# Half of a bf16 normalisation is moved from VectorE to GpSimd in an attention and expert kernel

## The chip, the cores and the metric

The kernel runs on all 8 cores of one Trainium2 chip. Each core takes one of the 8 batch entries (2048 tokens by 1024 features) with its own copy of the weights, and the cores exchange nothing. The metric is the device time in microseconds of the slowest core. The version before takes 1118.87 us (median of 3 runs, 1118.42 to 1119.35).

A core has TensorE (matmuls, PE in the profile), VectorE (DVE), ScalarE (ACT), GpSimd (POOL) and SyncE (SP, here only a DMA queue). They run their own instruction lists and meet at semaphores.

## What is computed

`x` is normalised over its features, and the result `xn` feeds two branches whose outputs are added to `x`:

```python
xn = layernorm(x)                                  # per token, over 1024 features
# branch 1: linear attention
q, k, v = split(xn @ w_qkv.T + b_qkv)              # 16 heads of 64
q = silu(q);  k = softmax(k, over tokens)
out = q @ (k.T @ v)                                # per head
out = layernorm(out) * sigmoid(gate(xn))
out = out @ w_out.T + b_out
# branch 2: 8 experts, top 2 by router logits xn @ Wr.T, capacity 769 tokens for each expert
y = x + out + sum over the chosen experts e of  w_e * (xn @ We[e])
```

## The kernel before

One function, `program(me, eng)`, is run once for each engine. It walks through the whole kernel in one order and emits only what belongs to the engine `me`, so the order of each engine's instructions is the order of the source. Helpers `mm` (TensorE, line 167), `dve` (VectorE, 177), `act` (ScalarE, 184), `gps` (GpSimd, 191) and `dma` (198) count the instructions, each of which raises its engine's semaphore when done; the parameter `inc` makes no difference in `dve`, `act` and `gps`. Each `dve`, `act` or `gps` instruction also waits until the one before it on its own engine has completed, and each `dma` until the one before it on its own queue has landed. `w(owner, ctr, val)` makes the engine `owner` wait for the counter `ctr`: "dv" is VectorE's, "gp" GpSimd's, "pe" TensorE's, "ac" ScalarE's, "d1" to "d3" the DMA queues.

The feature-major copy of `x` (8 chunks of 128 features by 2048 tokens) lies in `ar3` as bf16 (`xhi`). The stages, in order:

1. Load `x` and sum `x` and its square over the features by matmuls with a column of ones; router logits from `xhi` and a remainder `xlo3`.
2. Mean and 1/deviation of each token, as rows of 2048 numbers on one partition (`srow`, `qrow`, `crow`, `drow`). Then `reps[:, 0, :]` (scale) and `reps[:, 1, :]` (shift) are those rows spread to 128 partitions.
3. **The normalisation** (lines 342 to 352): for each of 4 blocks `tb` of 512 tokens and each of 8 chunks `h`, two VectorE instructions on 128x512 bf16: `tmpb = xhi * scale`, then `xn = tmpb + shift`. 64 instructions. `tmpb` and `tmpb2` are the two halves of the small tile `scr_b` (128x1024); `xn` lies in `ar1`, `xhi` in `ar3`.
4. **The routing chain**. TensorE transposes the logits into bank 4 and sums the router weights into bank 6. VectorE copies the two out (`lraw`, `wrsum`), and these copies stand behind the normalisation in VectorE's list. TensorE then waits for both copies, makes one small matmul (`wrsum` spread over partitions) and goes on to K.
5. **K projection**: 16 token tiles `tc` of 128 tokens, each as 2 banks of 9 matmuls (8 with `xn` as the stationary operand, one for the bias). A tile waits for its token block of `xn` by `t_xn_tb[tc // 4]`. ScalarE takes the exponential out of PSUM.
6. V projection, K^T V, Q projection, gate hidden layer, attention output, second layernorm, gate, output projection; then 8 experts of 256 matmuls each.
7. GpSimd adds `x` to each finished token tile (128x1024, f32), and ScalarE's queue writes it to `y`.

On GpSimd's queue the last four DMAs ahead of stage 3's end are `wk_t`, `wv_t`, `wg1_t` and `wg2_t`. Behind them stands a clearing of `scr_b` that waits for the whole normalisation, then a small memset, and then nothing until the load of `wq_t`, which waits for the end of K.

Of the kernel before, what the change touches and what calls it, by code (L numbers as in the profile page):

```python
# [9 lines left out]
ALU = mybir.AluOpType  # L10
# [4 lines left out]
HC = 8  # L15
# [7 lines left out]
def build_nc():  # L23
# [24 lines left out]
    with contextlib.ExitStack() as ctx:  # L48
# [31 lines left out]
        reps = sb("reps", [128, 2, 2048], BF16)  # L80
        scr_b = sb("scr_b", [128, 1024], BF16)
        tmpb = scr_b[:, 0:512]
        tmpb2 = scr_b[:, 512:1024]
# [40 lines left out]
        with nc.psum_tensor("PS", [128, 4096], F32) as PS:  # L124
# [8 lines left out]
            def bank(b, lo=0, hi=512):  # L133
                return PS[:, 512 * b + lo: 512 * b + hi]

            xn = ar1[:].rearrange("p (c t) -> p c t", c=HC)
            xhi = ar3[:].rearrange("p (c t) -> p c t", c=HC)
# [17 lines left out]
            def program(me, eng):  # L155
                c = {"pe": 0, "dv": 0, "ac": 0, "gp": 0, "d1": 0, "d2": 0, "d3": 0}
# [4 lines left out]
                def w(owner, ctr, val=None):  # L161
                    if me == owner:
                        eng.wait_ge(S[ctr], c[ctr] if val is None else val)

                def mm(out, l, r, start, stop, inc=False):
                    if me == "tensor":
                        i = eng.matmul(out, l, r, start=start, stop=stop)  # L167
                        if inc:
                            i.then_inc(S["pe"], 1)
                    if inc:  # L170
                        c["pe"] += 1
                    return c["pe"]

                def dve(name, *a, inc=True, **k):
                    if me == "vector":
                        eng.wait_ge(S["dv"], c["dv"])  # L176
                        getattr(eng, name)(*a, **k).then_inc(S["dv"], 1)  # L177
                    c["dv"] += 1
                    return c["dv"]

                def act(name, *a, inc=True, **k):
                    if me == "scalar":
                        eng.wait_ge(S["ac"], c["ac"])
                        getattr(eng, name)(*a, **k).then_inc(S["ac"], 1)  # L184
                    c["ac"] += 1
                    return c["ac"]

                def gps(name, *a, inc=True, **k):
                    if me == "gpsimd":
                        eng.wait_ge(S["gp"], c["gp"])  # L190
                        getattr(eng, name)(*a, **k).then_inc(S["gp"], 1)  # L191
                    c["gp"] += 1
                    return c["gp"]
# [84 lines left out]
                for h in range(HC):  # L278
                    for tb in range(TB):
                        sl = slice(512 * tb, 512 * (tb + 1))  # L280
# [35 lines left out]
                for which, rowsrc in ((0, drow), (1, crow)):  # L316
                    for tb in range(TB):
                        if which == 1 and tb == 0:
                            w("tensor", "dv", t_rows)
                        if t_reps_toks:  # L320
# [3 lines left out]
                           inc=True)  # L324
# [5 lines left out]
                t_reps = c["dv"]  # L330
# [10 lines left out]
                               ALU.subtract)  # L341
                t_xn_tb = []
                w("vector", "dv", t_reps)
                for tb in range(TB):
                    sl = slice(512 * tb, 512 * (tb + 1))
                    for h in range(HC):
                        dve("tensor_tensor", tmpb[:, :], xhi[:, h, sl],
                            reps[:, 0, sl], ALU.mult, inc=False)
                        dve("tensor_tensor", xn[:, h, sl], tmpb[:, :],
                            reps[:, 1, sl], ALU.add, inc=(h == HC - 1))  # L350
                    t_xn_tb.append(c["dv"])
                t_xn = c["dv"]
                w("gpsimd", "dv", t_xn)
                t_kvz = gps("memset", scr_b[:, :], 0.0)

# [54 lines left out]
                for tc in range(NT):  # L410
                    for ob in range(2):
                        idx = tc * 2 + ob
                        bnk = idx % 4
                        if idx == 0:
                            w("tensor", "dv", t_lgt_ev)
                            w("tensor", "d2", t_wk)
                        w("tensor", "dv", t_xn_tb[tc // 4])
                        if idx >= 4:
                            w("tensor", "ac", tok_k[idx - 4])
                        for h in range(HC):  # L420
                            mm(bank(bnk), xn[:, h, 128 * tc:128 * (tc + 1)],
                               wkv[:, 0, h, 512 * ob:512 * (ob + 1)],
                               start=(h == 0), stop=False)
                        mm(bank(bnk), ones_b[0:1, 0:128],
                           bk_sb[:, 512 * ob:512 * (ob + 1)], start=False,
                           stop=True, inc=True)
                        tk = c["pe"]
                        w("scalar", "pe", tk)
                        tok_k[idx] = act("activation",
                                         expK[:, tc, 512 * ob:512 * (ob + 1)],  # L430
                                         bank(bnk), AF.Exp)
# [11 lines left out]
                   inc=True)  # L443
# [12 lines left out]
                for tc in range(NT):  # L456
# [30 lines left out]
                    inc=False)  # L487
# [17 lines left out]
                for ch in range(HC):  # L505
# [12 lines left out]
                    for tc in range(NT):  # L518
                        mm(bank(b2, 0, 1), expK[:, tc, 128 * ch:128 * (ch + 1)],
                           ones_c_b[:, 0:1], start=(tc == 0), stop=(tc == NT - 1),  # L520
                           inc=(tc == NT - 1))
# [134 lines left out]
                for which, rowsrc in ((0, drow), (1, crow)):  # L656
                    for tb in range(TB):
                        if t_reps2_toks:
# [3 lines left out]
                           inc=True)  # L662
# [10 lines left out]
                for oc in range(HC):  # L673
                    for tb in range(TB):
# [16 lines left out]
                        sl = slice(512 * tb, 512 * (tb + 1))  # L691
# [17 lines left out]
                for tc in range(NT):  # L709
                    for ob in range(2):  # L710
# [8 lines left out]
                        for h in range(HC):  # L719
# [5 lines left out]
                           inc=True)  # L725
# [21 lines left out]
                for e_i in range(E):  # L747
                    src = accA if e_i % 2 == 0 else accB
                    dstv = accB if e_i % 2 == 0 else accA
                    for tc in range(NT):  # L750
                        for ob in range(2):
# [7 lines left out]
                            for h in range(HC):  # L759
# [3 lines left out]
                                   inc=(h == HC - 1))  # L763
# [31 lines left out]
            with nc.Block() as block:  # L795
                @block.tensor
                def _(eng):
                    program("tensor", eng)

                @block.vector  # L800
                def _(eng):
                    program("vector", eng)

                @block.scalar
                def _(eng):
                    program("scalar", eng)

                @block.sync
                def _(eng):
                    program("sync", eng)  # L810

                @block.gpsimd
                def _(eng):
                    program("gpsimd", eng)
# [44 lines left out]
```

## Time and profile before

| | |
|---|---|
| time, median of 3 | 1118.87 us |
| the profiled execution's own time | 1118.52 us |
| its span on the slowest core (core 2) | 1116.6 us |
| TensorE matmul busy | 874.3 us (78%) |
| VectorE busy | 453.2 us (41%) |
| ScalarE busy | 103.6 us (9%) |
| GpSimd busy | 58.0 us (5%) |
| spans of the eight cores | 1111.9 to 1116.6 us |
| mean granted TensorE clock, die 0 and die 1 | 0.864 and 0.866 |

The span runs from the first to the last instruction of the core; 1.9 us of the profiled execution's time lie outside it. A share of busy time is a mean over stages with different limits, so the rows further below are read stage by stage. GpSimd's durations are rough.

### The profile page before, as it was taken

Reading aid. Unit: us, or ns where it says so; the run is one execution under the profiler, and the core shown is the slowest. Engines: PE = TensorE matmul, PEld = TensorE weight load, DVE = VectorE, ACT = ScalarE, POOL = GpSimd, SP = SyncE. Lnnn points to the kernel's source line nnn. Section 1 sums busy time; section 2 is a strip of 40 time slices with the busy share of each in tenths; the row PEclk is TensorE's granted clock in tenths of the full one; section 3 lists DMA queues with packets and bytes.
Section 4 is the critical chain, followed back from the end, with each engine's and each line's share of the span. In section 5 each row is a group of like instructions: output and inputs, shape, how many; then the busy total and the mean of one; then the engine's idle time right before and its main releaser. Section 6 shows DMA issues by size and latency. Waiting matters only on the chain.

```text
span 1116.6 us, 11121 instructions; the slowest of 8 cores (1111.9 to 1116.6 us)
## 1 busy us (share of the span) xinstructions
PE 874.3 (78%) x3848; PEld 358.6 (32%) x3914; DVE 453.2 (41%) x692; ACT 103.6 (9%) x123; POOL 58.0 (5%) x58
## 2 busy tenths in 40 slices
PE   2338109999959995605549999999999999999992
PEld 0003003333353331101003334444444444444441
DVE  1248672023320007276763334444444444444441
ACT  1221002220002210512220000000000000000000
POOL 1011000000000000000000000000000000000244
PEclk8669559999958995855559999999999999999996
DMA  6844600030040022000000040404040404040376
GB/s 133 217 104 76 123 0 1 1 60 16 1 77 1 1 36 40 0 0 1 0 0 1 1 75 1 75 2 76 1 76 1 76 1 76 1 76 1 95 236 235
DMA packets 23300, 55.59 MB, mean 50 GB/s; under 512 B 4752, under 2 KB 4752, under 8 KB 22224
## 3 DMA queue, kind: packets, MB, share of 16 engines
q0 software_dynamic: 16160, 29.68, 16.5%
q1 hardware_dynamic: 4208, 12.63, 3.8%
q10 hardware_dynamic: 2880, 12.58, 3.0%
q8 instruction: 33, 0.54, 0.2%
q14 instruction: 19, 0.16, 0.0%
HBM read 76.18 MB, written 8.39 MB: 76 GB/s over the span
## 4 chain that ended last, share of the span: by engine, by line
PE 64%; DVE 17%; DMA 11%; issue 4%; ACT 2%; DVEq 1%; POOL 0%; POOLq 0%; ACTq 0%
PE PS L167 64%; DMA ar<-x_fm 6%; DMA y<-fpool 5%; DVE scr_b L177 5%; DVE ar L177 5%; DVE srow L177 3%; DVE reps L177 1%; ACT bpool L184 1%; DVE qrow L177 1%; ACT qrow L184 1%; DVEq L176 1%; DVE drow L177 0%; DVE crow L177 0%; DVE bpool L177 0%; DVE fpool L177 0%
## 5 line engine op out<-in xcount | busy, mean ns | idle before, releaser
L167 PE MATMUL PS<-ar 128*128 128x512 bf16 (+1 forms) x3135 | 700.0, 378 | 25.9 <-DVE ar L177 9.2
L167 PEld LDWEIGHTS PS<-ar 128*128 128x128 bf16 x3200 | 304.0, 100 | 386.3 <-issue 56.1
L177 DVE SCALAR_TENSOR_TENSOR ar<-PS,lc,ar 128x512 bf16<-128x512 f32 x256 | 192.2, 751 | 251.0 <-PE PS L167 251.0
L177 DVE CAST ar<-PS 128x512 bf16<-128x512 f32 x96 | 66.4, 692 | 94.2 <-PE PS L167 90.2
L167 PE MATMUL PS<-ar,ones_c_b 128*1 128x512 bf16 x64 | 23.2, 500 | 57.5 <-ACT bpool L184 57.2
L184 ACT ACTIVATE ar<-PS 128x512 bf16<-128x512 f32 x64 | 38.2, 597 | 93.7 <-PE PS L167 93.7
L198 POOL DMA_DIRECT2D ar<-we x8 | 7.0, 876 | 672.4 <-PE PS L167 672.4
L177 DVE TENSOR_TENSOR ar<-fpool,ar 128x2048 bf16<-128x2048 f32 x8 | 18.3, 2292 | 56.5 <-DMA ar<-x_fm 28.3
L167 PE MATMUL PS<-bpool,wg_sb 64*128 64x512 bf16 x32 | 18.7, 584 | 28.4 <-DVE ar L177 28.4
L167 PE MATMUL PS<-drow,ones_b 1*128 1x512 bf16 x8 | 4.4, 554 | 44.1 <-DVE crow L177 35.2
L191 POOL TENSOR_TENSOR fpool<-ar,fpool 128x1024 f32<-128x1024 bf16 x16 | 34.2, 2139 | 90.8 <-DVE ar L177 62.0
L184 ACT ACTIVATE bpool<-ar 128x2048 bf16<-128x2048 bf16 x16 | 30.6, 1910 | 86.2 <-DMA ar<-x_fm 48.2
L167 PE MATMUL PS<-bias_b,ones_b 1*128 1x512 bf16 x96 | 37.1, 387 | 0.3
L167 PE MATMUL PS<-ones_b,bias_a 1*128 1x512 bf16 (+1 forms) x68 | 33.2, 488 | 0.1
L177 DVE CAST bpool<-PS 64x512 bf16<-64x512 f32 x4 | 2.7, 682 | 75.1 <-PE PS L167 75.1
L177 DVE TENSOR_TENSOR scr_b<-ar,reps 128x512 bf16<-128x512 bf16 x64 | 27.2, 425 | 9.4 <-ACT bpool L184 2.5
L167 PEld LDWEIGHTS PS<-ar,ones_c_b 128*1 128x1 bf16 x64 | 5.3, 94 | 73.9 <-issue 71.9
L184 ACT ACT_TABLE_LOAD x6 | 7.7, 1283 | 222.5 <-PE PS L167 210.2
L177 DVE RECIPROCAL srow<-qrow 1x2048 f32<-1x2048 f32 x2 | 25.9, 12942 | 5.9 <-ACT qrow L184 5.9
L167 PE MATMUL PS<-wrsum_t,ones_f 1*128 1x8 f32 x2 | 0.6, 352 | 33.3 <-DVE wrsum_t L177 33.3
L177 DVE TENSOR_SCALAR w1c<-w0c 128x16 f32<-128x16 f32 x1 | 0.2, 176 | 64.1 <-ACT w0c L184 64.1
L167 PE MATMUL PS<-ar,wr_hi 128*8 128x512 bf16 x64 | 20.5, 400 | 6.9 <-DMA bias_b<-bk 6.9
(109 smaller groups left out, 288.2 us busy)
## 6 DMA issues: line engine op xcount, KB each, us to landing
ar<-we POOLq DMA_DIRECT2D x8, 2048.0 KB, 16.1
fpool<-x_tm SPq DMA_DIRECT2D x16, 512.0 KB, 4.2
y<-fpool ACTq DMA_DIRECT2D x16, 512.0 KB, 4.3
ar<-x_fm POOLq DMA_DIRECT2D x8, 512.0 KB, 7.0
fpool<-x_fm ACTq DMA_DIRECT2D x4, 1024.0 KB, 7.3
fpool<-x_fm SPq DMA_DIRECT2D x4, 1024.0 KB, 8.7
ar<-wk_t POOLq DMA_DIRECT2D x1, 2048.0 KB, 15.3
ar<-wv_t POOLq DMA_DIRECT2D x1, 2048.0 KB, 14.3
```

What stands on the lines that cost most here:

```text
L167: i = eng.matmul(out, l, r, start=start, stop=stop)
L176: eng.wait_ge(S["dv"], c["dv"])
L177: getattr(eng, name)(*a, **k).then_inc(S["dv"], 1)
L184: getattr(eng, name)(*a, **k).then_inc(S["ac"], 1)
L191: getattr(eng, name)(*a, **k).then_inc(S["gp"], 1)
L198: eng.dma_start(out=out, in_=in_).then_inc(S[q], 16)
```

## The change

The token blocks `tb` = 0 and 2 of the normalisation stay on VectorE with `tmpb` as scratch. The blocks 1 and 3 go to GpSimd, with `tmpb2` as scratch, and GpSimd waits for the complete `reps`. Each entry of `t_xn_tb` now names the counter too, and the K projection waits on it. `t_xn_gp` is not used further.

```diff
                 t_xn_tb = []
                 w("vector", "dv", t_reps)
+                w("gpsimd", "dv", t_reps)
                 for tb in range(TB):
                     sl = slice(512 * tb, 512 * (tb + 1))
+                    op = dve if tb % 2 == 0 else gps
+                    scr = tmpb if tb % 2 == 0 else tmpb2
                     for h in range(HC):
-                        dve("tensor_tensor", tmpb[:, :], xhi[:, h, sl],
-                            reps[:, 0, sl], ALU.mult, inc=False)
-                        dve("tensor_tensor", xn[:, h, sl], tmpb[:, :],
-                            reps[:, 1, sl], ALU.add, inc=(h == HC - 1))
-                    t_xn_tb.append(c["dv"])
+                        op("tensor_tensor", scr[:, :], xhi[:, h, sl],
+                           reps[:, 0, sl], ALU.mult, inc=False)
+                        op("tensor_tensor", xn[:, h, sl], scr[:, :],
+                           reps[:, 1, sl], ALU.add, inc=(h == HC - 1))
+                    t_xn_tb.append(("dv" if tb % 2 == 0 else "gp", c["dv" if tb % 2 == 0 else "gp"]))
                 t_xn = c["dv"]
+                t_xn_gp = c["gp"]
                 w("gpsimd", "dv", t_xn)
                 t_kvz = gps("memset", scr_b[:, :], 0.0)
...
-                        w("tensor", "dv", t_xn_tb[tc // 4])
+                        w("tensor", t_xn_tb[tc // 4][0], t_xn_tb[tc // 4][1])
```

GpSimd's list from the DMA of `wg1_t` to the load of `wq_t`, of the kernel before. `ar` stands for `ar1` to `ar4`, `wg_sb` for the two gate weights, `srow` for the small row that the second memset clears.

```order
L198 DMA wg_sb<-wg_t 128x8x64 [waits s_d2]
L198 DMA wg_sb<-wg_t 64x1024 [waits s_d2]
L191 MEMSET scr_b 128x1024 [waits s_dv,s_gp]
L191 MEMSET srow 1x8 [waits s_dv,s_gp]
L198 DMA ar<-wq_t 128x8x1024 [waits s_pe,s_d2]
```

The same stretch of the changed kernel; where the line of dots stands the two rows repeat until there are 32 TENSOR_TENSOR.

```order
L198 DMA wg_sb<-wg_t 128x8x64 [waits s_d2]
L198 DMA wg_sb<-wg_t 64x1024 [waits s_d2]
L191 TENSOR_TENSOR scr_b<-ar,reps 128x512 [waits s_dv,s_gp]
L191 TENSOR_TENSOR ar<-scr_b,reps 128x512 [waits s_gp]
...
L191 MEMSET scr_b 128x1024 [waits s_dv,s_gp]
L191 MEMSET srow 1x8 [waits s_dv,s_gp]
L198 DMA ar<-wq_t 128x8x1024 [waits s_pe,s_d2]
```

32 instructions have come in ahead of the clearing of `scr_b`; the first waits for VectorE's count at the end of `reps`, the others only for GpSimd's own.

VectorE's list at the end of the normalisation, which is the same text in both kernels: before, these two TENSOR_TENSOR are the last of 64, now the last of 32.

```order
L177 TENSOR_TENSOR scr_b<-ar,reps 128x512
L177 TENSOR_TENSOR ar<-scr_b,reps 128x512
L177 COPY lraw<-PS 128x128
L177 COPY wrsum_t<-PS 1x8
L177 COPY wr_rep<-PS 128x8
```

The copies to `lraw` and `wrsum_t` that TensorE waits for before K follow right behind the last of VectorE's own blocks, whatever GpSimd has done by then.

TensorE's waits at the start of the fifth K tile (token block 1), one piece of the difference:

```order
 L167 MATMUL PS<-bias_b,ones_b 128x512
+L167 MATMUL PS<-ar 128x512 [waits s_gp,s_ac]
+L167 MATMUL PS<-ar 128x512 x7
+L167 MATMUL PS<-bias_b,ones_b 128x512
```

TensorE now waits for GpSimd's counter at the tiles 4 to 7 and 12 to 15, where it waited for VectorE's.

## Rows read from the trace of the kernel before

**Rows 1.** Chain that ended last, end of normalisation: start us, us, what.

```profile
165.31 0.43 DVE scr_b L177
165.84 0.43 DVE ar L177
166.37 0.30 DVE lraw L177
166.93 0.25 issue
167.18 0.58 PE PS L167 x2
168.09 13.05 PE PS L167 x49
```

**Rows 2.** Who waited for whom, 125 to 170 us: total, times, longest.

```profile
POOL scr_b L191 <- DVE ar L177: 34.4, 1, 34.4
PE PS L167 <- DVE wrsum_t L177: 33.3, 1, 33.3
```

**Rows 3.** Stages from normalisation into V: stretch, length, busy of each engine, clock, DMA.

```profile
core 2: us, PE busy (x) PEld busy (x) DVE busy (x) ACT busy (x) POOL busy (x), PEclk, DMA share, GB/s
132.00:166.40 34.40, 1.46 (x48) 1.37 (x48) 27.27 (x66) 0.00 (x0) 0.04 (x1) 0.50 0.12 35
168.00:172.00 4.00, 3.93 (x12) 1.35 (x12) 2.75 (x13) 0.51 (x1) 0.00 (x0) 0.66 0.00 0
172.00:180.00 8.00, 8.00 (x35) 2.92 (x34) 3.16 (x13) 3.17 (x5) 0.00 (x0) 1.00 0.00 1
180.00:240.00 60.00, 59.64 (x248) 22.12 (x252) 0.00 (x0) 17.90 (x29) 0.92 (x1) 1.00 0.00 1
240.00:308.00 68.00, 66.80 (x277) 24.82 (x282) 25.12 (x50) 0.33 (x2) 0.17 (x1) 1.00 0.19 32
```

**Rows 4.** Instruction groups by shape, 132 to 166.4 us, VectorE.

```profile
L177 DVE TENSOR_TENSOR ar<-scr_b,reps 128x512 bf16<-128x512 bf16 x32 | 13.6, 425 | 3.7 <-DVE scr_b L177 0.5
L177 DVE TENSOR_TENSOR scr_b<-ar,reps 128x512 bf16<-128x512 bf16 x32 | 13.6, 425 | 3.3
```

**Rows 5.** Timeline of VectorE and TensorE: start us, us, engine, line, operation.

```profile
129.76 2.28 DVE L177 TENSOR_TENSOR bpool<-fpool,bpool 8x2048 bf16<-8x2048 f32 x1
132.15 0.43 DVE L177 TENSOR_TENSOR scr_b<-ar,reps 128x512 bf16<-128x512 bf16 x1
132.68 0.43 DVE L177 TENSOR_TENSOR ar<-scr_b,reps 128x512 bf16<-128x512 bf16 x1
...
165.84 0.42 DVE L177 TENSOR_TENSOR ar<-scr_b,reps 128x512 bf16<-128x512 bf16 x1
166.37 0.29 DVE L177 COPY lraw<-PS 128x128 f32<-128x128 f32 x1
167.18 0.56 PE L167 MATMUL PS<-wrsum_t,ones_f 1*128 1x8 f32 x2 [33.31 <-DVE wrsum_t L177]
168.07 1.91 PE L167 MATMUL PS<-ar 128*128 128x512 bf16 x4 [0.33 <-DVE wr_rep L177]
```

**Rows 6.** Timeline of GpSimd around the normalisation, and its first memsets.

```profile
1.12 0.53 POOL L191 MEMSET ones_b<- 128x512 bf16 x1 [0.42 <-POOLq L24]
1.77 0.21 POOL L191 MEMSET ones_f<- 128x128 f32 x1
...
131.48 0.56 POOL L198 DMA_DIRECT2D wg_sb<-wg_t  x1 [2.84 <-DMA wg_sb<-wg_t]
166.45 0.95 POOL L191 MEMSET scr_b<- 128x1024 bf16 x1 [34.41 <-DVE ar L177]
167.52 0.10 POOL L191 MEMSET srow<- 1x8 f32 x1
238.62 0.92 POOL L198 DMA_DIRECT2D ar<-wq_t  x1 [71.00 <-PE PS L167]
```

**Rows 7.** GpSimd's adds and VectorE's expert accumulations beside them, then the adds alone.

```profile
L177 DVE SCALAR_TENSOR_TENSOR ar<-PS,lc,ar 128x512 bf16<-128x512 f32 x27 | 20.3, 751 | 26.4 <-PE PS L167 26.4
L191 POOL TENSOR_TENSOR fpool<-ar,fpool 128x1024 f32<-128x1024 bf16 x12 | 25.7, 2141 | 83.1 <-DVE ar L177 62.0 <-DMA y<-fpool 21.2
L191 POOL TENSOR_TENSOR fpool<-ar,fpool 128x1024 f32<-128x1024 bf16 x4 | 8.5, 2131 | 7.6 <-DMA y<-fpool 7.6
```

**Rows 8.** Timeline of TensorE, two banks of the K projection.

```profile
233.64 1.90 PE L167 MATMUL PS<-ar 128*128 128x512 bf16 x8
235.47 0.38 PE L167 MATMUL PS<-bias_b,ones_b 1*128 1x512 bf16 x1
235.79 1.90 PE L167 MATMUL PS<-ar 128*128 128x512 bf16 x8
```

**Rows 9.** Busy time of each engine in the expert stage and at its end.

```profile
652.00:1046.00 394.00, 391.09 (x1785) 177.92 (x1820) 170.78 (x228) 0.00 (x0) 6.13 (x7) 1.00 0.23 38
1046.00:1091.50 45.50, 45.24 (x207) 20.63 (x211) 19.73 (x27) 0.00 (x0) 22.57 (x11) 1.00 0.67 211
```

## The prediction, made before the changed kernel ran

> **What bounds the kernel now.** I read the chain that ended last first, since a change in one stage is worth only what it moves on that chain. Around the normalisation the chain lies wholly on VectorE: its last two TENSOR_TENSOR of the normalisation, the copy to `lraw`, a small matmul, and at 168.09 us the K projection [rows 1]. Then the waits of that stretch: TensorE waits 33.3 us in one piece for `wrsum_t`, a copy that stands behind the normalisation in VectorE's list, and GpSimd waits 34.4 us to clear `scr_b` [rows 2]. Then the busy time by stage: from 132.0 to 166.4 us TensorE does 1.46 us of work and GpSimd next to none; from 172 us on TensorE is full (59.64 of 60 us from 180 to 240) [rows 3]. So one engine works, one that matters waits, and each microsecond taken from VectorE here is a microsecond by which K starts earlier.
>
> Does that microsecond reach the end? Behind K, TensorE's own work or a chain started by it sets the pace: 66.80 of 68 us in V [rows 3], 391.09 of 394 us in the experts [rows 9], and the loads of later weights are tied to TensorE's counts, as `wq_t` at 238.62 us, released by the end of K [rows 6]. Nothing later is tied to an absolute time. The weights of K and V have landed before 132 us (the DMA of `wg2_t`, behind both in a serial queue, issues at 131.48 us [rows 6]). I take a shift of K's start as a shift of the end, one for one.
>
> **The part that is removed.** The 64 instructions start at 132.15 us and the last ends at 165.84 + 0.42 = 166.26 us: 34.1 us [rows 5], which is 64 x 425 ns = 27.2 us of work [rows 4] and about 0.10 us between two, because each waits for the one before (132.68 - 132.15 = 0.53 us from start to start [rows 5]). With 32 left, and nothing else changed, VectorE needs 32 x 0.53 = 17.0 us, and the stage is 17.1 us shorter. This is the most that the change can give.
>
> The step from the last VectorE instruction to K stays: 168.07 - 166.26 = 1.8 us [rows 5]. I cost it at nothing. It has two PSUM copies, one small matmul and one more copy.
>
> **The part that is added on GpSimd.** 32 instructions on 128x512 bf16. The trace has none of them. The nearest row is the final add, 128x1024, at 2141 ns [rows 7]; half of it is 1.07 us. GpSimd's spans follow the number of elements: the memset of 512 columns takes 0.53 us and that of 1024 takes 0.95 [rows 6], which leaves about 0.11 us that does not scale and would make it (2.14 - 0.11)/2 + 0.11 = 1.12 us. From end to start two GpSimd instructions that wait for each other are 0.12 us apart (1.12 + 0.53 to 1.77 [rows 6]). So by itself GpSimd needs 1.2 us each, 16 x 1.2 = 19 us for token block 1 and 38 us for both. Bounds of one instruction: 0.53 us from below (the memset of that size), 2.14 us from above (the add of double size).
>
> GpSimd can begin at once: its last DMA instruction ends at 131.48 + 0.56 = 132.04 us [rows 6], and `reps` was complete long before VectorE's 129.76 us row [rows 5]. Queued behind the new work are only the clearing of `scr_b`, a memset of 8 numbers and the load of `wq_t`, which is released at 238.6 us. The clearing is needed only in K^T V. All of it hides under K, which ends after 238 us; with a delay of up to 20 us nobody waits for it.
>
> **The waits that are added on TensorE.** Tiles 4 to 7 and 12 to 15 wait for GpSimd. A bank of K takes 235.79 - 233.64 = 2.15 us [rows 8], so a token block (8 banks) takes 17.2 us; the first one is about 1.4 us longer, since the granted clock is 0.66 in the first 4 us (a mix of 1.2 and 2.4 GHz) after 0.50 during the wait [rows 3]. If VectorE were undisturbed, K would start at 132.15 + 17.0 + 1.8 = 151.0 us, want block 1 at about 169.5 and block 3 at about 204; GpSimd would have them at 132.1 + 19 = 151 and 170 us. Block 1 becomes late only above 37/16 = 2.3 us for each GpSimd instruction. Behind such a wait the whole of TensorE's list would stand. At 1.2 us the two waits cost nothing. The clock is at 0.50 through the wait of 33 us [rows 3], and a wait some 15 us longer or shorter still ends at that level, so the slow start of K stays.
>
> **The part that decides: do the two engines run side by side?** Each VectorE instruction here reads two tensors from SBUF, and so does each GpSimd instruction. The trace has the two engines busy together only at the end: GpSimd's adds take 2141 ns beside VectorE's accumulations and 2131 ns alone, and the accumulations keep 751 ns [rows 7], but those read one tensor from PSUM and only one from SBUF. The DMA instruction at 131.48 us also lies beside a two-tensor VectorE instruction (129.76 + 2.28 us) [rows 5, 6], but computes nothing. So no row shows the pairing that the change makes. Bounds:
> - no interference: 32 x 0.53 = 17.0 us on VectorE, a change of -17.1 us.
> - strict turns, where only one of the two engines runs at a time and they alternate: each VectorE instruction costs 0.425 + 1.07 = 1.495 us, 32 of them 47.8 us, a change of 47.8 - 34.1 = +13.7 us. With both handovers added (0.10 + 0.12 us) and 1.12 us for GpSimd it is 1.77 us, 56.6 us, +22.5 us. With a GpSimd instruction of 0.53 us it would be 0.955 us, 30.6 us, -3.5 us.
>
> By rows alone these ends are open. The undisturbed pair at the end [rows 7] is the nearest row, yet it leaves out just what is new, the second SBUF tensor on VectorE. I take strict turns at 1.495 us: a second SBUF stream on each side is the one resource that both need here and that no row shows shared, so the undisturbed pair counts for little, and I give interference of some kind four chances in five.
>
> The Trainium skill bears on this. "SBUF — State Buffer", section "Who interferes with whom", says that a VectorE instruction with two SBUF inputs takes its second one through a read interface that it shares with GpSimd, and that this is an exclusive lock held for a whole instruction, so that the later one waits fully; a VectorE instruction with one SBUF input, outside the two-port modes, does not collide. By that rule the sum is the one with turns, without it -17.1 us; rows 7 agree with its second half (751 and 2141 ns undisturbed), and no row of this trace shows its first half.
>
> **Sum.** 1118.52 us (the profiled execution, which has 1.9 us outside its span of 1116.6) + 13.7 = 1132.2 us; against the median, which is 0.35 us higher, 1132.6. I say 1132.5. In the terms of the stage: VectorE's pitch from start to start decides, with the break-even at 34.1/32 = 1.07 us. Below that pitch the kernel is faster, above it slower.
>
> **The rivals.**
> 1. *No interference.* K starts at 151.0 us. For it: the undisturbed pair at the end [rows 7], and GpSimd idle for 34.4 us with room for the work [rows 2]. Against it: those rows have one SBUF tensor on VectorE's side. Time 1118.9 - 17.1 = 1101.8 us. Here GpSimd may even be held back until VectorE is done (VectorE first each time): block 1 would then be ready at 149.2 + 19 = 168 us, just before K wants it, and the time is the same. Chance 0.20.
> 2. *Partial sharing*, where both engines stretch but overlap. If a VectorE instruction doubles to 0.85 us and keeps its gap, the pitch is 0.95 us: 30.4 us, -3.7 us; at 0.70 us it is a pitch of 0.80 and -8.5 us. Or GpSimd's instruction is shorter than half the large one, down to the -3.5 us above. For it: GpSimd takes 2.09 ns per column (2141/1024) and VectorE 0.83 (425/512), so the slower side may leave room for the faster one. About 1113 us. Chance 0.11, of which 0.04 falls within 0.2% (about 2.2 us, what a measurement of this kernel can tell from no change).
> 3. *GpSimd late.* VectorE is undisturbed but a bf16 GpSimd instruction takes 3 us: block 1 is ready at 180 instead of 169.5 us, block 3 at 228 when K wants it at about 215, so -17.1 + 10.5 + 13 = +6 us, 1125 us. Against it: it would be more than the 2.14 us of an add of twice the columns. Chance 0.03.
> 4. *Turns, but with a pitch near 1.07 us*, so that what is halved comes back exactly. Within 0.2%. Chance 0.04.
> The forecast, strict turns with a pitch of 1.35 to 1.8 us, has 0.62, with its own range of 1128 to 1141 us.
>
> **Chances and range.** Faster by over 0.2%: 0.20 + 0.07 = 0.27. Within: 0.04 + 0.04 = 0.08. Slower: 0.62 + 0.03 = 0.65. The case on the other side has a fifth of the chance by itself, so the range has to reach down to it: 1101 to 1140 us.
>
> **What the new profile would show.** Forecast right: VectorE's TENSOR_TENSOR of 128x512 in the normalisation show 1.3 to 1.7 us from start to start, either as longer durations or as gaps, and GpSimd's 32 are spread over the same stretch; both end within 2 us of each other at about 180 us; K starts at about 182 us; TensorE has no wait for GpSimd; from K to the end every stage is as long as before, and all stages before 132 us too. Rival 1: VectorE stays at 425 ns and 0.53 us, its last instruction ends near 149 us. Rival 2: durations of 0.6 to 0.9 us. Rival 3: TensorE waits for GpSimd's `ar` at tile 4. The step from normalisation to K should remain 1.8 us in all of them. The forecast is wrong if the pitch is under 1.07 us, and the one-for-one step is wrong if the time moves by another amount than K's start.

## The result and the profile after

The changed kernel takes 1125.42 us against 1118.91 us before (medians of 10 runs each); the ratio of the two is 1.0056 with a 95% interval of 1.0045 to 1.0066. It is slower, by 6.3 us (0.56%), where +13.6 us had been forecast. The sign and the place were right, and the loss was less than half of the forecast one. 1125.42 us lies inside the range of 1101 to 1140 us, which had been stretched to hold the opposite outcome too, and outside the forecast's own range of 1128 to 1141 us. (Executions in which one half of the chip ran at a visibly lower clock, two of the ten of the changed kernel among them, are left out of this ratio, of all ratios and times below and of the table; without them the changed kernel's median is 1125.0 us.)

VectorE's timeline in the normalisation, changed kernel, core 7, which is the slowest; as in [rows 5], start us, us, engine, line, operation:

```profile
133.18 0.42 DVE L177 TENSOR_TENSOR scr_b<-ar,reps 128x512 bf16<-128x512 bf16 x1
133.71 0.43 DVE L177 TENSOR_TENSOR ar<-scr_b,reps 128x512 bf16<-128x512 bf16 x1
134.24 0.42 DVE L177 TENSOR_TENSOR scr_b<-ar,reps 128x512 bf16<-128x512 bf16 x1
134.77 1.26 DVE L177 TENSOR_TENSOR ar<-scr_b,reps 128x512 bf16<-128x512 bf16 x1
136.13 1.18 DVE L177 TENSOR_TENSOR scr_b<-ar,reps 128x512 bf16<-128x512 bf16 x1
137.42 1.19 DVE L177 TENSOR_TENSOR ar<-scr_b,reps 128x512 bf16<-128x512 bf16 x1
138.71 1.19 DVE L177 TENSOR_TENSOR scr_b<-ar,reps 128x512 bf16<-128x512 bf16 x1
...
171.00 1.19 DVE L177 TENSOR_TENSOR ar<-scr_b,reps 128x512 bf16<-128x512 bf16 x1
172.29 0.29 DVE L177 COPY lraw<-PS 128x128 f32<-128x128 f32 x1
```

GpSimd's, same core; the rows of [rows 6] had nothing between 132.04 and 166.45 us:

```profile
134.00 0.56 POOL L198 DMA_DIRECT2D wg_sb<-wg_t  x1 [2.82 <-DMA wg_sb<-wg_t]
134.57 1.16 POOL L191 TENSOR_TENSOR scr_b<-ar,reps 128x512 bf16<-128x512 bf16 x1
135.88 1.16 POOL L191 TENSOR_TENSOR ar<-scr_b,reps 128x512 bf16<-128x512 bf16 x1
137.18 1.15 POOL L191 TENSOR_TENSOR scr_b<-ar,reps 128x512 bf16<-128x512 bf16 x1
138.47 1.15 POOL L191 TENSOR_TENSOR ar<-scr_b,reps 128x512 bf16<-128x512 bf16 x1
...
173.34 1.15 POOL L191 TENSOR_TENSOR scr_b<-ar,reps 128x512 bf16<-128x512 bf16 x1
174.64 1.15 POOL L191 TENSOR_TENSOR ar<-scr_b,reps 128x512 bf16<-128x512 bf16 x1
```

Read the two together. Until GpSimd starts, VectorE works as before: 0.42 us, every 0.53 us. From GpSimd's first instruction on, VectorE's same instruction is recorded at 1.19 us (the first one at 1.26), and the next starts 1.29 us later. That is GpSimd's distance from start to start too (137.18 to 138.47); below, this distance is called the pitch. Each VectorE instruction ends 0.28 us after a GpSimd one has ended (137.42 + 1.19 = 138.61; 137.18 + 1.15 = 138.33): it has been held while GpSimd's instruction ran. GpSimd is not held at all: its pitch of 1.29 us stays the same after VectorE has left (173.34 to 174.64 us lies behind VectorE's last normalisation instruction, which ends at 172.19).

VectorE's 32 instructions took 172.19 - 133.18 = 39.0 us on this core, against 34.1 for 64 before [rows 5]. TensorE's wait answers to [rows 2], in the waits of 125 to 240 us, again total, times, longest:

```profile
PE PS L167 <- DVE wrsum_t L177: 38.4, 1, 38.4
```

On core 0 GpSimd was free before VectorE. Its first instruction met VectorE's two-input subtraction of the logits and was itself the one that was held, 2.53 instead of 1.15 us. Core 0, GpSimd:

```profile
127.81 2.53 POOL L191 TENSOR_TENSOR scr_b<-ar,reps 128x512 bf16<-128x512 bf16 x1
130.48 1.15 POOL L191 TENSOR_TENSOR ar<-scr_b,reps 128x512 bf16<-128x512 bf16 x1
```

and VectorE:

```profile
127.05 2.28 DVE L177 TENSOR_TENSOR bpool<-fpool,bpool 8x2048 bf16<-8x2048 f32 x1
129.43 1.19 DVE L177 TENSOR_TENSOR scr_b<-ar,reps 128x512 bf16<-128x512 bf16 x1
```

There VectorE's part took 41.2 us (32 x 1.29). In this execution the cores 0, 2, 4 and 6 lose these 7.1 us and the others 4.9. Core 7 sets the time here, but of the eight executions that the ratio rests on the slowest core was an even-numbered one in five, and only this execution has a trace. So how the two losses mix in the median is not shown; the measured change of about 6.3 us lies between them.

### The profile page after: what moved, and what is told of

Same layout as the page of the kernel before. It is cut to its first block, busy times and chain, and to the rows that moved or that the text cites. A ratio compares the mean times of both kernels' runs of the same rounds, so it can differ in the third digit from the quotient of the medians.

```text
span 1122.6 us, 11188 instructions; the slowest of 8 cores (1117.5 to 1122.6 us)
## 1 busy us (share of the span) xinstructions
PE 882.0 (79%) x3914; PEld 359.1 (32%) x3914; DVE 462.4 (41%) x660; ACT 103.6 (9%) x123; POOL 95.5 (9%) x90
## 4 chain that ended last, share of the span: by engine, by line
PE 65%; DVE 18%; DMA 11%; issue 3%; ACT 2%; DVEq 1%; POOL 0%; POOLq 0%; ACTq 0%
PE PS L167 65%; DMA ar<-x_fm 6%; DVE scr_b L177 6%; DMA y<-fpool 5%; DVE ar L177 5%; DVE srow L177 3%; DVE reps L177 1%; ACT bpool L184 1%; DVE qrow L177 1%; ACT qrow L184 1%; DVEq L176 1%; DVE drow L177 0%; DVE crow L177 0%; DVE bpool L177 0%; DVE fpool L177 0%
## 5 line engine op out<-in xcount | busy, mean ns | idle before, releaser
L177 DVE TENSOR_TENSOR scr_b<-ar,reps 128x512 bf16<-128x512 bf16 x48 | 31.1, 647 | 7.4 <-ACT bpool L184 2.5
```

## The experiments

The theory after this reading: **lockstep**. A VectorE instruction with two SBUF inputs is held until the GpSimd instruction that reads SBUF is about done, then runs, and its own work mostly fits into the changeover to GpSimd's next instruction. So VectorE passes one instruction for each of GpSimd's, at GpSimd's own pitch. The rivals: a shared bandwidth (size matters, count does not), a collision over something else than reading, and a trouble of GpSimd's work as such.

One table first, since all runs answer one question too: does the end follow the start of K? The second column is the time from VectorE's first instruction of the normalisation to the small matmul in front of K, on the slowest core, less the 167.18 - 132.15 = 35.0 us of before [rows 5]; the third is the median time less the median of before, measured on the same chip.

| run | stage, us | time, us |
|---|---|---|
| changed kernel | +5.1 (core 7), +7.3 (core 0) | +6.1 |
| GpSimd in halves | -9.3 | -8.0 |
| GpSimd in doubles | +10.5 | +12.1 (two runs) |
| VectorE operand in PSUM | -8.7 | -8.9 |
| GpSimd memsets | -17.1 | -17.2 |
| GpSimd after VectorE | -17.1 | -18.0 |
| routing part first | -25.8 | -26.0 |
| the same, with the split | -15.8 | -16.1 |
| VectorE in doubles | -10.6 | -10.1 |
| GpSimd copies | -11.0 | -11.8 |
| GpSimd one block only | +4.0 | +3.5 |

The end follows within 1.6 us in all of them. (The second column is one core of one execution, the third a median of executions, so they cannot agree exactly.)

**GpSimd's instructions in halves.**

```diff
+                    np_ = 1 if tb % 2 == 0 else 2
+                    wd = 512 // np_
                     for h in range(HC):
+                        for p_ in range(np_):    # slices of wd columns
...
```

> The changed kernel, but each GpSimd instruction of the normalisation is cut into two of 256 columns (64 instructions instead of 32); VectorE's 32 of 512 columns are untouched. Theory 1 (one VectorE instruction passes per GpSimd instruction, whatever its size): GpSimd's pitch falls from 1.29 to about (1.15-0.11)/2+0.11+0.14 = 0.77 us, VectorE follows at 0.77 us, its part takes 32 x 0.77 = 25 us instead of 39 to 41, K starts about 15 us earlier than in the changed kernel: about 1110 us, faster than before. Rival (the engines share a bandwidth, or VectorE is slowed by a factor for as long as GpSimd works): VectorE keeps its pitch of 1.29 us, about 1125 us.

Measured: 1110.76 us, ratio 0.9927 (0.991 to 0.9943): the same work for GpSimd in twice as many instructions turns the loss into a gain. Groups by shape, 126 to 215 us (count, busy us, mean ns, idle before); GpSimd, then VectorE:

```profile
L191 POOL TENSOR_TENSOR ar<-scr_b,reps 128x256 bf16<-128x256 bf16 x32 | 21.3, 666 | 4.9 <-POOL scr_b L191 0.4
L177 DVE TENSOR_TENSOR ar<-scr_b,reps 128x512 bf16<-128x512 bf16 x16 | 10.7, 670 | 1.7
```

GpSimd's instruction takes 0.67 us, its pitch is 0.81 us, and VectorE's untouched instruction shrinks from 1.19 to 0.70 us at the same pitch of 0.81 us (138.40 to 139.21 us). A shared bandwidth would have left it alone.

**GpSimd's instructions in doubles.** The blocks 1 and 3 in one instruction, through a view of `[128, 2, 512]` elements, with `bpool2` as scratch.

> The changed kernel, but GpSimd handles its two token blocks together in 16 instructions of 1024 columns (scratch in another free tile). Theory 1: one VectorE instruction per GpSimd instruction of about 2.2+0.14 = 2.33 us: 16 x 2.33 = 37 us for 16 VectorE instructions, then 16 free ones at 0.53 us = 8.5, together 46 us instead of 39 to 41: about 1130 us. Rival (shared bandwidth): the same bytes move, VectorE at a pitch of 1.29 us throughout, 1125 us.

Measured: 1130.20 and 1131.67 us; of four runs only these two can be compared, so there is no interval. Start us, us of VectorE's rows:

```profile
141.14 2.15 DVE L177 TENSOR_TENSOR scr_b<-ar,reps 128x512 bf16<-128x512 bf16 x1
143.40 2.15 DVE L177 TENSOR_TENSOR ar<-scr_b,reps 128x512 bf16<-128x512 bf16 x1
...
176.82 0.42 DVE L177 TENSOR_TENSOR ar<-scr_b,reps 128x512 bf16<-128x512 bf16 x1
```

The pitch is 2.26 us while GpSimd works, and 0.42 us is back when it is done. One VectorE instruction of 512 columns costs 0.81, 1.29 or 2.26 us, by the size of its neighbour's. GpSimd's scratch is another tile here (`bpool2`), so the tile `scr_b`, of which both engines use a half in the changed kernel, is not the cause.

**VectorE's instructions in doubles**, the counterpart: blocks 0 and 2 in 16 instructions, GpSimd as in the changed kernel.

> The changed kernel, but VectorE handles its two token blocks together in 16 instructions of 1024 columns (scratch in another free tile); GpSimd's 32 are untouched. Theory 1 (one VectorE instruction per GpSimd instruction, and VectorE's reading fits into the pause between two of them only if it is short): 16 instructions at a pitch of 1.3 to 1.7 us, 21 to 27 us instead of 39 to 41, and GpSimd's pitch stretched by what VectorE needs beyond the pause: 1107 to 1112 us. Rival (shared bandwidth): the same bytes at the same rate, 16 x 2.6 = 41 us, about 1125 us.

Measured: 1110.34 us, ratio 0.9911 (0.9896 to 0.9927). VectorE's first row, which runs before GpSimd has begun, two later ones, and two of GpSimd's:

```profile
132.73 0.69 DVE L177 TENSOR_TENSOR bpool<-ar,reps 128x1024 bf16<-128x1024 bf16 x1
...
140.78 1.45 DVE L177 TENSOR_TENSOR bpool<-ar,reps 128x1024 bf16<-128x1024 bf16 x1
142.34 1.45 DVE L177 TENSOR_TENSOR ar<-bpool,reps 128x1024 bf16<-128x1024 bf16 x1
```

```profile
144.94 1.41 POOL L191 TENSOR_TENSOR ar<-scr_b,reps 128x512 bf16<-128x512 bf16 x1
146.50 1.41 POOL L191 TENSOR_TENSOR scr_b<-ar,reps 128x512 bf16<-128x512 bf16 x1
```

Now GpSimd is held too: its pitch grows from 1.29 to 1.56 us, by 0.27 us, and a VectorE instruction of 1024 columns is longer than one of 512 by 0.69 - 0.425 = 0.27 us. So in the changed kernel VectorE's 0.425 us hid whole in the changeover, and at 1024 columns all that exceeds it is paid. Only these two sizes were run. This is the number that the prediction lacked.

**VectorE's second operand from PSUM.**

```diff
+                        r0 = bank(7)[:, :] if tb % 2 == 0 else reps[:, 0, sl]
+                        r1 = bank(7)[:, :] if tb % 2 == 0 else reps[:, 1, sl]
```

> The changed kernel, but VectorE's 32 instructions take their second operand from PSUM (bank 7, so the values of token blocks 0 and 2 are other ones); GpSimd's are untouched. If VectorE collides only through its second SBUF input: its durations are those of one undisturbed instruction (about 0.7 us, pitch 0.8 us), its part takes 26 us, K starts some 14 us earlier than in the changed kernel, about 1111 us. Rival (VectorE collides with GpSimd through its SBUF write or its first read): pitch stays 1.29 us, about 1125 us.

Measured: 1109.95 us, ratio 0.9925 (0.9908 to 0.9942). VectorE's first instruction, then GpSimd and VectorE side by side in groups of 126 to 215 us:

```profile
131.72 0.69 DVE L177 TENSOR_TENSOR scr_b<-ar,PS 128x512 bf16<-128x512 bf16 x1
```

```profile
L191 POOL TENSOR_TENSOR ar<-scr_b,reps 128x512 bf16<-128x512 bf16 x16 | 18.4, 1150 | 2.3
L177 DVE TENSOR_TENSOR scr_b<-ar,PS 128x512 bf16<-128x512 bf16 x16 | 11.0, 687 | 1.7
```

All 32 VectorE instructions take 687 ns, the first, ahead of GpSimd's start at 133.21 us, as well as those beside it. With one SBUF input and an SBUF output VectorE is not held; with two SBUF inputs it is. The PSUM form is slower alone (687 against 425 ns) and faster in company.

**GpSimd only writes.**

```diff
+                            gps("memset", scr[:, :], 0.0)
+                            gps("memset", xn[:, h, sl], 0.0)
```

> The changed kernel, but GpSimd only writes: memsets of 128x512 in place of its 32 TENSOR_TENSOR, so token blocks 1 and 3 of xn are zero. If the collision is over reading SBUF: VectorE keeps 425 ns and 0.53 us, 17 us for its part, K starts 22 to 24 us earlier than in the changed kernel, about 1102 us. Rival (the collision is over writing, or over the engine as such): VectorE's pitch follows the memset's, 0.53+0.12 = 0.65 us, 21 us, about 1106 us, with durations of about 0.55 us instead of 0.425; the durations tell them apart better than the time.

Measured: 1101.64 us, ratio 0.9849 (0.9833 to 0.9864).

```profile
L191 POOL MEMSET ar<- 128x512 bf16 x16 | 8.4, 524 | 1.9
L177 DVE TENSOR_TENSOR ar<-scr_b,reps 128x512 bf16<-128x512 bf16 x16 | 6.8, 425 | 1.7
```

VectorE is at its 425 ns. A GpSimd instruction that only writes does not hold it.

**GpSimd copies, one input instead of two.**

```diff
+                            gps("tensor_copy", scr[:, :], xhi[:, h, sl])
+                            gps("tensor_copy", xn[:, h, sl], scr[:, :])
```

> The changed kernel, but GpSimd's 32 TENSOR_TENSOR become copies of 128x512 bf16 (one SBUF input instead of two), so token blocks 1 and 3 of xn are the plain bf16 input. Theory (a GpSimd instruction that reads SBUF holds VectorE back for its own length, whatever it computes): VectorE's pitch is GpSimd's own, copy length plus 0.14 us, as long as that is over 0.53 us; a copy of 0.5 to 0.8 us gives a pitch of 0.65 to 0.95 us and VectorE's part 21 to 30 us. Rival (only GpSimd's two-input instructions collide): VectorE at 425 ns and 0.53 us, 17 us, about 1102 us.

Measured: 1108.05 us, ratio 0.9898 (0.988 to 0.9916). VectorE and GpSimd:

```profile
139.32 0.65 DVE L177 TENSOR_TENSOR ar<-scr_b,reps 128x512 bf16<-128x512 bf16 x1
140.07 0.64 DVE L177 TENSOR_TENSOR scr_b<-ar,reps 128x512 bf16<-128x512 bf16 x1
```

```profile
139.08 0.62 POOL L191 COPY ar<-scr_b 128x512 bf16<-128x512 bf16 x1
139.82 0.62 POOL L191 COPY scr_b<-ar 128x512 bf16<-128x512 bf16 x1
```

One SBUF input on GpSimd's side is enough to hold VectorE, by the copy's length: pitch 0.75 us on both, and VectorE's record again ends 0.27 us behind GpSimd's.

**One block on GpSimd** (`tb < 3` in place of `tb % 2 == 0`).

> VectorE does token blocks 0 to 2, GpSimd block 3 alone, started at once as in the changed kernel. Theory (each GpSimd instruction holds one VectorE instruction for 1.29 instead of 0.53 us, and takes one of 0.53 us off VectorE's list): VectorE's part is 16 x 1.29 + 32 x 0.53 = 37.6 us, +3.5 us against before (half of the changed kernel's loss), 1121 to 1123 us. Rival (the loss comes from a fixed cost of the split, such as the first GpSimd instruction or the shared scratch tile): as much as in the changed kernel, 1125 us, or a gain of 8 us for a quarter less on VectorE.

Measured: 1123.39 us, ratio 1.0034 (1.0021 to 1.0047). VectorE's pitch is 1.29 us beside GpSimd's 16 instructions and 0.53 us after them:

```profile
153.01 1.19 DVE L177 TENSOR_TENSOR ar<-scr_b,reps 128x512 bf16<-128x512 bf16 x1
154.30 1.19 DVE L177 TENSOR_TENSOR scr_b<-ar,reps 128x512 bf16<-128x512 bf16 x1
155.59 0.42 DVE L177 TENSOR_TENSOR ar<-scr_b,reps 128x512 bf16<-128x512 bf16 x1
156.12 0.42 DVE L177 TENSOR_TENSOR scr_b<-ar,reps 128x512 bf16<-128x512 bf16 x1
```

Half the moved work, about half the loss: each instruction moved saves VectorE 0.53 us and costs another one 1.29 - 0.53 = 0.76 us. VectorE's part is 172.24 - 134.15 = 38.1 us where 37.6 were expected, so a fixed price, if there is one, is not above about 0.5 us.

**GpSimd after VectorE**, blocks 2 and 3.

```diff
+                    if tb == 2:
+                        w("gpsimd", "dv", t_xn_tb[1][1])
```

> VectorE does token blocks 0 and 1, GpSimd blocks 2 and 3, and GpSimd waits until VectorE has finished its two. The work of each engine is that of the changed kernel; only the overlap is gone. If the loss of the changed kernel is the overlap alone: VectorE 32 x 0.53 = 17 us, K starts at about 151 us, GpSimd at a pitch of 1.29 us has block 2 at 149+21 = 170 us (wanted at about 187) and block 3 at 191 us (wanted at about 204), TensorE never waits for it: 1119-17 = about 1102 us. Rival (GpSimd's instruction itself is the trouble, for example slower while TensorE runs, or disturbing K): over 1106 us, with TensorE waiting for GpSimd or a longer K.

Measured: 1102.46 us, ratio 0.9844 (0.9828 to 0.986). Both engines do what they do in the changed kernel, not at the same time. VectorE has 425 ns, GpSimd the same 1.15 us beside TensorE's K, and in the waits from 152 to 225 us TensorE has none for GpSimd:

```profile
149.56 0.42 DVE L177 TENSOR_TENSOR ar<-scr_b,reps 128x512 bf16<-128x512 bf16 x1
```

```profile
150.19 1.15 POOL L191 TENSOR_TENSOR scr_b<-ar,reps 128x512 bf16<-128x512 bf16 x1 [15.44 <-DVE ar L177]
151.48 1.15 POOL L191 TENSOR_TENSOR ar<-scr_b,reps 128x512 bf16<-128x512 bf16 x1
```

This is the gain that the split can give, the 17.1 us of the prediction's rival 1: the stage is shorter by just that, and the time by 18.0 us.

**The routing part first**, all on VectorE. What K waits for last is `wrsum`, not `xn`, so the copies were moved ahead.

```diff
                     t_xn_tb.append(c["dv"])
+                    if tb == 0:
+                        w("tensor", "dv", t_lgt_hl)
...
+                        t_lraw_ev = dve("tensor_copy", lraw[:], bank(4)[:, 0:128])
...
+                        t_wr_ev = dve("tensor_copy", wrsum[:, :], bank(6)[0:1, 0:E])
...
+                        t_wrr_ev = dve("tensor_copy", wr_rep[:], bank(4)[:, 0:E])
```

> The kernel before, all on VectorE, with one thing moved: the router transposes, the router weight sums and their three copies stand behind token block 0 instead of behind block 3, so K waits for block 0 only. If K's start is what the end hangs on, one for one: K starts 25.4 us earlier (48 x 0.53), less about 1 us for VectorE's wait on the small matmul, which now stands between blocks: about 1094 us. If instead the later blocks become the limit (VectorE has block 3 at about 168 us, K wants it at 195), or a later stage does not follow: between 1094 and 1119 us with a TensorE wait for VectorE in K.

Measured: 1094.48 us, ratio 0.9768 (0.9752 to 0.9783), the fastest of all, without GpSimd.

```profile
141.58 0.29 DVE L177 COPY lraw<-PS 128x128 f32<-128x128 f32 x1
141.97 0.15 DVE L177 COPY wrsum_t<-PS 1x8 f32<-1x8 f32 x1
142.38 0.56 PE L167 MATMUL PS<-wrsum_t,ones_f 1*128 1x8 f32 x2 [7.55 <-DVE wrsum_t L177]
142.88 3.59 PE L167 MATMUL PS<-ar 128*128 128x512 bf16 x8
143.12 0.17 DVE L177 COPY wr_rep<-PS 128x8 f32<-128x8 f32 x1 [1.00 <-PE PS L167]
143.40 0.42 DVE L177 TENSOR_TENSOR scr_b<-ar,reps 128x512 bf16<-128x512 bf16 x1
```

TensorE's wait of 33.3 us [rows 2] is down to 7.6, and blocks 1 to 3 are made under K. The waits of 141 to 215 us show no other wait of TensorE for VectorE.

**The same with the split**: the edit of the run before it, made in the changed kernel.

> The changed kernel with the routing part behind token block 0, as in the run before it. Theory (lockstep at GpSimd's pitch of 1.29 us): block 0 takes 16 x 1.29 = 20.7 us instead of 8.5, so K starts 12 us later than without the split: about 1106 us, faster than before but slower than the same order without GpSimd. Rival (the split costs nothing once the routing part is out of the way): equal to the run without the split, about 1094 us.

Measured: 1104.35 us, ratio 0.9864 (0.9847 to 0.9882). Faster than before, and 9.9 us slower than the same order without GpSimd: the price of the overlap is now paid on block 0 alone. Block 0 took 18.4 us (134.40 to 152.76) instead of the expected 20.7, because on this core GpSimd began 1.4 us after VectorE (135.81 against 134.40 us), and VectorE's first three instructions were free: 3 x 0.76 = 2.3 us.

## Why the prediction was half right

- *K hangs on VectorE's list, and the end on K's start.* Right. The table above shows it from -26 to +12 us.
- *The part removed*, 32 x 0.53 = 17.0 us left, -17.1 us. Right: it is met to 0.1 us in the stage where GpSimd does not hold VectorE (memsets, GpSimd after VectorE).
- *GpSimd's instruction*, 1.07 to 1.12 us and 1.2 us from start to start. Slightly low: 1.15 and 1.29 us. That it ends in time for K was right; TensorE never waited for it.
- *That the two interfere*, taken against the undisturbed pair of [rows 7]. Right, and the experiments name the cause. The Trainium skill's rule ("SBUF — State Buffer", "Who interferes with whom": a two-SBUF-input VectorE instruction and a GpSimd instruction that reads SBUF exclude each other, for a whole instruction) agrees in each case tried as to who holds whom: the PSUM operand (687 ns beside GpSimd and ahead of it), the memset (425 ns), the copy (0.64 us) and the order of arrival (2.53 us on core 0). In one point the records differ from the rule, as far as GpSimd's rough durations can tell: VectorE's record (to 138.61 us) and GpSimd's next (from 138.47 us) overlap by 0.14 us, and GpSimd's is not longer for it.
- *The price of a turn*, the step that failed: "each VectorE instruction costs 0.425 + 1.07 = 1.495 us". Measured: 1.29 us. I summed two recorded durations, VectorE's and GpSimd's, and left GpSimd's pause out. A turn costs GpSimd's own pitch, which is there anyway, plus only that part of VectorE's work that does not fit into the changeover: nothing at 512 columns, 0.27 us at 1024. Luck made the error smaller: 0.425 us too much for VectorE was partly made up by 0.22 us too little for GpSimd (1.07 instead of 1.29). The sum would have been 32 x 1.29 - 34.1 = +7.2 us, or +4.9 us on the cores where GpSimd starts late, against the +13.7 us forecast and +6.3 measured. With my own estimate of GpSimd's pitch (1.2 us) it would have been +4.3 us. The chances had a hole here too: rival 4 stands for pitches within about 0.07 us of 1.07 (0.2% of the time), the forecast starts at 1.35, nothing was put between, and the measured 1.29 us lies there. (The forecast's upper end of 1.8 us is +23.5 us, 1142 and not 1141 us.) Mostly for the same reason K started at 173.8 us on core 7 and not at 182.
- *Clock and start of K.* Right as far as the sum needs it: in the changed kernel the first eight matmuls of K take 3.59 us and the next eight 1.90 us, after a wait at a granted clock of 0.50 (135 to 173 us).

What stays open: what exactly fills the 0.28 us between the end of GpSimd's record and that of VectorE's, which is less than the 0.425 us that VectorE's instruction takes alone. The runs show how much work hides at the changeover (512 columns, and not 1024), not why. GpSimd's durations are rough, so the 0.28 us are too.

## What to carry to other kernels

Before work is moved to an idle GpSimd, look at the operands, not at the idle time: a VectorE instruction with two SBUF inputs beside a GpSimd instruction that reads SBUF runs at the pitch of GpSimd's instruction, so a split into halves pays only where GpSimd's pitch is less than twice VectorE's, here 1.06 us (0.75 and 0.81 paid, 1.29 did not), or where the two do not overlap, or one VectorE operand is in PSUM. (That run used whatever lay in a PSUM bank; what it costs to put the real operand there was not measured.) And read what the waiting engine waits for last: here it was a copy of 8 numbers queued behind 64 long instructions, and moving it was worth 26 us, more than the whole split could have given.

## What the runs showed of the hardware that had not been expected

- A held instruction is recorded as a long one, not as idle time: VectorE's busy time rises from 453.2 to 462.4 us though half of its normalisation is gone, and its 0.425 us read as 1.19 us. Busy time is no measure of work here.
- GpSimd's TENSOR_TENSOR on bf16 took 0.67 us for 256 columns, 1.15 for 512 and 2.12 for 1024, about 0.19 us plus 1.9 ns for each column, and 0.14 us from the end of one to the start of the next; a copy of 512 columns took 0.62 us and a memset 0.52.
- Cutting the neighbour's instructions in two makes VectorE faster (1.19 to 0.70 us) though GpSimd then needs longer in all (64 x 0.81 = 52 us against 32 x 1.29 = 41 us).
